# Expert weights of a token stored beside its row and fetched with it, in a kernel of attention and a routed expert layer

## The chip, the cores and the metric

The kernel runs on one core of one Trainium2 chip. The metric is the device time of one execution in microseconds (us).

## What is computed

The input is x, 2 sequences of 2048 tokens with 256 values each, float32. First comes attention with 16 heads of 16 values (softmax over all keys, the causal mask applied after it), added to x and layer-normalised: h. Then the expert layer with 8 experts, two for each token:

```
probs = softmax(h @ router_weight.T);  the two largest, divided by their sum = the weights of a token
each expert keeps at most capacity = 1280 of its tokens, those with the largest weights
kept_w = weight / sum of the kept weights of the token
out[token] = sum over its two experts of kept_w * ((pre * silu(gate)) @ ff_post_act_weight[e].T)
result = layernorm(h + out)
```

With pre and gate the products of the token's row with two 256 x 1024 matrices of the expert.

## The kernel before, in words

**Attention (up to 1034 us of the trace)** is not touched. It leaves x + attention in `x_sb`, 128 partitions by 32 token tiles by 256. Rows of the first sequence are normalised there and stored by SyncE (SP) to `h_dram` (the rows that experts gather) and `acc_dram` (the rows onto which results are added). Both are 4096 x 256 float32.

**Routing (1034 to 1067 us).** ScalarE (ACT) normalises the second sequence and splits the first expert's up weights into two parts for exact products (L1548 on). SP stores the second sequence's rows (L1242, L1243). VectorE (DVE) works through `route` (L1683 on), a chain of small dependent instructions: the two picks of each token (`pick`, one-hot over 8 experts for 32 token tiles), its weights (`kept_w`, L1711), the place of each token in its expert's list (`prefixes`, `places`), and then whether some expert has more than 1280 tokens (`flag`). If it has, a further branch of every engine runs; here it doesn't run. GpSimd (POOL) makes the constant tables, clears a part of y and copies the first expert's down weights (L1288), and then waits.

**The list (1067 to 1094 us).** `slot_row` says for each slot of each expert which token stands in it, 128 partitions by 80 columns (8 experts by 10 tiles of slots); `slot_w` has the token's weight. Both come out of one-hot products, in 8 pieces of 8 token tiles, with two buffers of each operand: DVE makes `in_q` (L1676: which of 80 columns) and `in_p` (L1677: which partition), DVE multiplies `in_q` by the token number into one half of `marks` (L1681), ACT multiplies it by the weight into the other half, eight instructions for a piece (L1536), and TensorE (PE) adds up `in_p` transposed times `marks` (L1388), 128 x 160 float32, eight products of two passes for a piece. The semaphore `list_ready` hands the buffers back to DVE (L1673) and ACT. After piece 8 DVE copies both halves out (L1795, L1796), and POOL, which waits for `slot_row` alone of these (L1309), gathers the first expert's rows with ten indirect DMAs (L1302), 128 rows each. PE begins the first expert when the first four have landed.

**The experts (1109 us to the end).** A loop over eight experts. For each, PE makes the up products in two groups of 512 slots and eight blocks f (L1431), ACT and DVE form the hidden rows, PE makes the down products (L1446), and DVE multiplies them by the slot's weight `wt2` while it copies them out (`leave`, L1866). POOL gathers the next expert's rows at the start of an expert and adds the results onto `acc_dram`. A third group with up to 256 slots runs for experts with over 1024 tokens. DVE sets `wt2` at an expert's start, from ten columns of `slot_w`, once `expert_over` has come (L1875 to L1877). At f = 4 (TURN_AT_F) of the first group, DVE takes the transposed rows of the second group (L1811), and at f = 5 it splits the down weights (L1805). The last expert has a branch of its own that normalises everything and stores it.

Of the kernel before, what the change touches and what calls it, by code (L numbers as in the profile page):

```python
# [4 lines left out]
FP32 = mybir.dt.float32  # L5
# [221 lines left out]
def program(nc, x_tok, x_T, wq, wk, wv, wr_T, w1_T, wg_T, w2_T, out):  # L227
    ctx = ExitStack()
    with ctx:
        def sem(name):  # L230
            return ctx.enter_context(nc.semaphore(name))

        def sb(stack, name, shape, dt=FP32):
            return stack.enter_context(nc.sbuf_tensor(name, shape, dt))
# [7 lines left out]
        v_dram = nc.dram_tensor("v_dram", (NGP, P, NT * VW), FP32).ap()  # L242
        h_dram = nc.dram_tensor("h_dram", (T, D), FP32).ap()
        acc_dram = nc.dram_tensor("acc_dram", (T, D), FP32).ap()
# [454 lines left out]
        acc_view = acc_dram.rearrange("(t p) d -> p t d", p=P)  # L699
        h_view = h_dram.rearrange("(t p) d -> p t d", p=P)  # L700
        stats = ctx.enter_context(nc.sbuf_tensor("stats", [P, TT, 6], FP32, side="right"))
# [48 lines left out]
        with ExitStack() as st, nc.Block() as block:  # L750
# [198 lines left out]
            def _(dve):  # L949
# [79 lines left out]
                for gg in range(NGP):  # L1029
                    for back, work, x, i in DVE_ORDER:  # L1030
# [8 lines left out]
                        if gg >= GPB and back == 0 and work == "sum" and x % 4 == 3 and measured < NT:  # L1039
                            if measured == 0:  # L1040
# [23 lines left out]
        over_ready, cand_ready, cand_count = sem("over_ready"), sem("cand_ready"), sem("cand_count")  # L1064
        places_ready, eq_ready, id_ready, wgt_ready, list_ready = (sem("places_ready"), sem("eq_ready"), sem("id_ready"), sem("wgt_ready"),
                                                                   sem("list_ready"))
        lists_read, more_ready = sem("lists_read"), sem("more_ready")
        PIECES = [(k, part) for part in range(TT // OHP) for k in range(TOPK)]
# [27 lines left out]
        with ExitStack() as st, nc.Block() as block:  # L1096
# [5 lines left out]
            xin_at = nc.sbuf_base  # L1102
            xin = [sb(st, f"xin{j}", [P, CT, D]) for j in range(2)]
            assert xin_at >= probs_at and nc.sbuf_base <= probs_at + 4 * P_RING * KSPAN
            y = [sb(st, f"y{j}", [P, CT, D]) for j in range(2)]
            slot_row = sb(st, "slot_row", [P, NSLOT], U32)
            slot_w = sb(st, "slot_w", [P, NSLOT])
            row = [sb(st, f"row{j}", [P, CT], U32) for j in range(2)]
# [35 lines left out]
            in_q = [sb(st, f"in_q{j}", [P, OHP, NSLOT]) for j in range(2)]  # L1144
            marks = [sb(st, f"marks{j}", [P, OHP, 2, NSLOT]) for j in range(2)]

# [34 lines left out]
            cand_ps = y_ps[:, 2, 0:E]  # L1181
            list_ps = y_ps[:, 3, 0:2 * NSLOT]
# [4 lines left out]
            others = xin[0]  # L1187
# [48 lines left out]
            def _(sp):  # L1236
# [5 lines left out]
                sp.dma_start(h_view[:, of_batch(1), :], x_sb[:, of_batch(1), :]).then_inc(h_stored, 16)  # L1242
                sp.dma_start(acc_view[:, of_batch(1), :], x_sb[:, of_batch(1), :]).then_inc(acc_stored, 16)  # L1243

                def body(i, j, prep):
# [25 lines left out]
            def _(pool):  # L1271
# [13 lines left out]
                def split_down(i, j):  # L1285
                    pool.wait_ge(r2_loaded, count(16, i, j, 16))
                    pool.sem_inc(pool_went_on, 1)
                    nc.gpsimd.tensor_copy(w2[0][:], raw2[:]).then_inc(w2_hi, 1)  # L1288

                split_down(0, 0)  # L1290

                def set_rows(j, e, rows_set):
# [15 lines left out]
                pool.wait_ge(acc_stored, 16 * B)  # L1308
                pool.wait_ge(lists_read, 1)  # L1309
                fetch(0, slot_row[:, 0:CT])  # L1310
# [70 lines left out]
            def _(pe):  # L1381
                def list_piece(n, round):

                    pe.wait_ge(id_ready, n + 1 + round * NP)
                    if round == 0:
                        pe.wait_ge(wgt_ready, OHP * (n + 1))
                    for t in range(OHP):
                        last = nc.tensor.matmul(list_ps, in_p[n % 2][:, t, :], marks[n % 2][:, t, :, :].rearrange("p v s -> p (v s)"),  # L1388
                                                start=(n == 0 and t == 0), stop=(t == OHP - 1), skip_group_check=True)
                    last.then_inc(list_ready, 1)  # L1390
# [120 lines left out]
            def _(act):  # L1511
# [17 lines left out]

                def weights(n):  # L1530
                    k, tiles = of_piece(n)
# [18 lines left out]
                for n in range(2 * DC):  # L1550
                    split_up_piece(n)
                for n in range(NP):
                    weights(n)

# [61 lines left out]
            def _(dve):  # L1616
# [51 lines left out]
                def mark(n, round):  # L1668

                    k, tiles = of_piece(n)  # L1670
                    at = n + round * NP
                    if at >= 2:
                        dve.wait_ge(list_ready, at - 1)  # L1673
                        if round == 0:
                            dve.wait_ge(wgt_ready, OHP * (at - 1))
                    nc.vector.tensor_tensor(in_q[n % 2][:], each(upward[:, 0:NSLOT], tiles), wide(at_q[:, k, tiles], NSLOT), ALU.is_equal).then_inc(eq_ready, 1)  # L1676
                    nc.vector.tensor_tensor(in_p[n % 2][:], each(upward, tiles), wide(at_p[:, k, tiles], P), ALU.is_equal)  # L1677
                    dve.wait_ge(eq_ready, at + 1)
                    if round == 1:
                        nc.vector.tensor_tensor(marks[n % 2][:, :, 1, :], in_q[n % 2][:], wide(kept_w[:, k, tiles], NSLOT), ALU.mult)  # L1680
# [62 lines left out]
                with dve.If(too_many > 0):  # L1743
                    link5 = chain(dve, dve5)

                    link5(nc.vector.tensor_tensor(wm[:], pick[0][:], wide(wgt[:, 0, :]), ALU.mult))
                    link5(nc.vector.tensor_tensor(work[:], pick[1][:], wide(wgt[:, 1, :]), ALU.mult))
# [40 lines left out]
                    weigh(link5, kept_w, kept_w, ALL)  # L1788
                    places(link5, ALL)
                    dve.wait_ge(places_ready, 2)  # L1790
# [79 lines left out]
                dve.wait_ge(y_cleared, 2)  # L1870
                dve.wait_ge(wt_set, 1)

                def body(i, j, prep):

                    dve.wait_ge(expert_over, i * 2 + (j + 1))  # L1875
                    nc.vector.tensor_copy(wt2[j][:], slot_w[:, bass.ds((i * 2 + j) * CT, CT)]).then_inc(wt_set, 1)
                    dve.wait_ge(wt_set, i * 2 + (j + 2))  # L1877
                    for g in range(2):
# [23 lines left out]
                        for f in range(FC + 1):  # L1902
# [72 lines left out]
```

## Time and profile before

| | |
|---|---|
| median of three runs | 1734.03 us (1733.4 to 1735.66) |
| the profiled execution's own time | 1735.2 us |
| its span in the trace | 1733.4 us |
| PE busy | 1622.3 us (94%) |
| ACT busy | 1255.3 us (72%) |
| DVE busy | 1141.7 us (66%) |
| POOL busy | 300.2 us (17%) |

The span is from the first to the last record of the trace; the 1.8 us between it and the time lie around it. Busy shares are averages over stages that have different limits, so the argument is made in the stages that the change touches, from the instructions in order of time. A "chain" is the sequence of work that ended last, followed back from the end.

### The profile page before, as it was taken

The numbers are of one execution on the slowest core, as the hardware profiler recorded it, in microseconds if no ns is written. First come the engines' busy times: TensorE is split into PE (matmuls) and PEld (weight loads), VectorE is DVE, ScalarE is ACT, GpSimd is POOL, SyncE is SP. The second block draws the span as 40 slices with busy tenths as digits, with TensorE's granted clock in tenths as the row PEclk, the third lists the DMA queues.
The fourth block names the chain that finished last, engine by engine and source line by source line (L and its number), as shares of the span: only waits on it lengthen the run. The fifth ranks groups of instructions, "written<-read, shape, count | busy, mean of one in ns | idle before, by whom it ended". The sixth has DMA issues, their size and how long they took to land. (4 is left out here: it accounts for less than half of the span.)

```text
span 1733.4 us, 31338 instructions
## 1 busy us (share of the span) xinstructions
PE 1622.3 (94%) x12878; PEld 951.5 (55%) x12878; DVE 1141.7 (66%) x1766; ACT 1255.3 (72%) x1350; POOL 300.2 (17%) x247
## 2 busy tenths in 40 slices
PE   8979999999999999999999993699999999999995
PEld 6723333333333333333333343589998988889984
DVE  7847687777776878777868778445454444644474
ACT  7869999999999999999999985233333333433333
POOL 1000000000000000000310000424243425425144
PEclk9979999999999999999999996899999999999998
DMA  7692030300300303003031002213142323323043
GB/s 258 209 256 67 1 88 1 78 11 2 88 1 1 88 1 78 11 2 88 1 100 48 1 26 97 98 38 107 15 112 65 69 57 68 100 50 90 5 134 121
DMA packets 78897, 118.29 MB, mean 68 GB/s; under 512 B 9202, under 2 KB 62811, under 8 KB 78734
## 3 DMA queue, kind: packets, MB, share of 16 engines
q1 hardware_dynamic: 63840, 98.32, 19.2%
q0 software_dynamic: 14880, 17.82, 5.8%
q8 instruction: 109, 1.79, 0.4%
q14 instruction: 36, 0.29, 0.1%
q10 hardware_dynamic: 32, 0.07, 0.0%
HBM read 80.22 MB, written 40.37 MB: 70 GB/s over the span
## 5 line engine op out<-in xcount | busy, mean ns | idle before, releaser
L973 DVE TENSOR_REDUCE sums<-expq 128x1 f32<-128x1536 f32 (+7 forms) x576 | 559.6, 1033 | 175.7 <-ACT expq L943 175.3
L943 ACT ACTIVATE probs<-scores 128x1536 f32<-128x1536 f32 (+1 forms) x384 | 509.2, 1478 | 12.3 <-PE scores L839 12.0
L943 ACT ACTIVATE expq<-scores 128x1536 f32<-128x1536 f32 x320 | 447.4, 1536 | 2.5 <-PE scores L839 0.9
L861 PE MATMUL o_ps<-probs,v 128*32 128x256 f32 (+1 forms) x4864 | 347.8, 368 | 0.0
L839 PE MATMUL scores<-aq,ak 98*128 98x512 bf16 (+3 forms) x1280 | 304.2, 353 | 12.4 <-PEq L620 10.9
L1594 ACT ACTIVATE gate<-up_ps 128x512 f32<-128x512 f32 x128 | 76.6, 599 | 326.3 <-PE up_ps L1431 315.7
L839 PE MATMUL scores<-ak,aq 98*128 98x512 bf16 (+3 forms) x1184 | 265.1, 343 | 22.7 <-ACT probs L943 16.9
L839 PEld LDWEIGHTS scores<-aq,ak 98*128 98x128 bf16 x1280 | 95.1, 98 | 216.6 <-ACT expq L943 75.5
L1431 PE MATMUL up_ps<-xeT_hi,wup_hi 128*128 128x512 f32 x512 | 202.9, 396 | 3.3 <-DVE xeT_lo L1811 1.4
L1907 DVE TENSOR_TENSOR mid<-up_ps,gate 128x512 f32<-128x512 f32 x128 | 88.4, 691 | 176.1 <-ACT gate L1594 171.0
L1431 PE MATMUL up_ps<-xeT_lo,wup_hi 128*128 128x512 f32 x512 | 202.5, 395 | 0.0
L1431 PE MATMUL up_ps<-xeT_hi,wup_lo 128*128 128x512 f32 x512 | 201.5, 393 | 0.0
L839 PEld LDWEIGHTS scores<-ak,aq 98*128 98x128 bf16 x1184 | 88.7, 98 | 198.8 <-ACT probs L943 91.0
L861 PEld LDWEIGHTS o_ps<-probs,v 128*32 128x32 f32 x4864 | 100.1, 108 | 170.0 <-issue 168.5
L1446 PE MATMUL y_ps<-w_hi,mid_hi 128*128 128x256 f32 x528 | 148.2, 281 | 0.0
L1446 PE MATMUL y_ps<-w_lo,mid_hi 128*128 128x256 f32 x528 | 147.5, 279 | 0.0
L1446 PE MATMUL y_ps<-w_hi,mid_lo 128*128 128x256 f32 x528 | 147.3, 279 | 0.0
L811 POOL TENSOR_TENSOR x_sb<-x_sb,attn 128x1024 f32<-128x1024 f32 x7 | 16.6, 2374 | 744.6 <-DVE attn L1004 744.6
L1352 POOL DMA_INDIRECT acc_dram<-y,row x70 | 110.0, 1571 | 126.6 <-DVE y L1866 80.4
L1431 PEld LDWEIGHTS up_ps<-xeT_hi,wup_hi 128*128 128x128 f32 x512 | 96.8, 189 | 25.5 <-DVE xeT_lo L1811 1.8
L1431 PEld LDWEIGHTS up_ps<-xeT_hi,wup_lo 128*128 128x128 f32 x512 | 96.8, 189 | 21.1
L1431 PEld LDWEIGHTS up_ps<-xeT_lo,wup_hi 128*128 128x128 f32 x512 | 96.7, 189 | 21.2
(268 smaller groups left out, 1903.6 us busy)
## 6 DMA issues: line engine op xcount, KB each, us to landing
raw<-w_T SPq DMA_DIRECT2D x16, 1024.0 KB
split_dram<-parts SPq DMA_DIRECT2D x48, 256.0 KB, 2.9
aq<-split_dram SPq DMA_DIRECT2D x42, 256.0 KB
ak<-split_dram SPq DMA_DIRECT2D x42, 256.0 KB
raw<-wg_T SPq DMA_DIRECT2D x8, 1024.0 KB
v_dram<-vst SPq DMA_DIRECT2D x8, 544.0 KB, 4.7
v<-v_dram SPq DMA_DIRECT2D x8, 544.0 KB, 10.6
xT<-x_T SPq DMA_DIRECT2D x8, 512.0 KB, 6.2
```

Of the source, the lines that this page charges most:

```text
L811: nc.gpsimd.tensor_tensor(cols, cols, attn[:], ALU.add).then_inc(attn_added, 1)
L839: last = nc.tensor.matmul(dst[:, at:at + w], still, moving[0:KS, h, lo:lo + w], start=True, stop=True, skip_group_check=True)
L861: last = nc.tensor.matmul(o_ps[g % O_RING][32 * h:32 * h + 32, col:col + w], value(gg, k, h, 32), probs[:, m % 2 * GH + h, at:at + w], sta ...
L943: nc.scalar.activation(dst, src[:, 0:w], ACT.Exp, scale=HD ** -0.5).then_inc(exp_done, 1)
L973: last = nc.vector.tensor_reduce(sums[:, gg % 2, col, h:h + 1], expq[:, at % X_RING, lo:lo + w], AX.X, ALU.add)
L1352: pool.indirect_dma_start(out=acc_dram[:, :], out_offset=bass.IndirectOffsetOnAxis(ap=row[j][:, t:t + 1], axis=0), in_=y[j][:, t, :], in_o ...
L1431: last = nc.tensor.matmul(up_ps[n % 2][:, k, 0:cols.stop - cols.start], wup[a][:, k, c, f * P:(f + 1) * P], x[b][:, c, cols], start=(c == ...
L1446: last = nc.tensor.matmul(y_ps[:, t, :], mid2[a][:, f, t * P:(t + 1) * P], w2[b][:, f, :], start=(f == 0 and t % 2 == 0 and (a, b) == PAIR ...
L1594: nc.scalar.activation(gate[f % 2][:], up_ps[f % 2][:, 0, :], ACT.Silu).then_inc(silu_done, 1)
L1907: nc.vector.tensor_tensor(mid[f % 2][:], up_ps[f % 2][:, 1, :], gate[f % 2][:], ALU.mult).then_inc(mul_done, 1)
```

## The change

`h_dram` gets eight more columns: a row is 264 values, 1056 bytes. The kept weights of a token are spread over eight columns by expert (`dense`), which takes three instructions on POOL, and one further DMA of SP writes them beside the rows, 4096 pieces of 32 bytes. A gathered row then brings its weight with it, and `wt2` is taken from the gathered tile, at f = 4 instead of at the expert's start. The list's products carry the token numbers alone, 80 columns instead of 160; ACT makes them in place of the weights, and DVE no longer multiplies. The first gather waits for `slot_row` and, through SP, for the weights to be in memory. The diff, cut to its core; what is left out besides is the branch for an expert with too many tokens, which does the same for its own weights:

```diff
-        h_dram = nc.dram_tensor("h_dram", (T, D), FP32).ap()
+        h_dram = nc.dram_tensor("h_dram", (T, D + E), FP32).ap()
...
-        h_view = h_dram.rearrange("(t p) d -> p t d", p=P)
+        h_rows = h_dram.rearrange("(t p) d -> p t d", p=P)
+        h_view, w_view = h_rows[:, :, 0:D], h_rows[:, :, D:D + E]
...
-            xin = [sb(st, f"xin{j}", [P, CT, D]) for j in range(2)]
+            xin = [sb(st, f"xin{j}", [P, CT, D + E]) for j in range(2)]
...
-            marks = [sb(st, f"marks{j}", [P, OHP, 2, NSLOT]) for j in range(2)]
+            marks = [sb(st, f"marks{j}", [P, OHP, NSLOT]) for j in range(2)]
+            dense, dense_1 = sb(st, "dense", [P, TT, E]), sb(st, "dense_1", [P, TT, E])
...
@@ SyncE, behind the stores of the second sequence's rows @@
+                sp.wait_ge(dense_ready, 4)
+                sp.dma_start(w_view, dense[:]).then_inc(h_stored, 16)
+                sp.wait_ge(over_ready, 1)
+                too_many = sp.value_load(flag[0:1, 1:2], min_val=0, max_val=1)
+                sp.wait_ge(h_stored, 16 * (B + 1))
...
+                sp.sem_inc(rows_known, 1)
...
@@ GpSimd, behind the copy of the first down weights @@
+                pool.wait_ge(dense_ready, 1)
+                nc.gpsimd.tensor_tensor(dense[:], pick[0][:], wide(kept_w[:, 0, :]), ALU.mult).then_inc(dense_ready, 1)
+                nc.gpsimd.tensor_tensor(dense_1[:], pick[1][:], wide(kept_w[:, 1, :]), ALU.mult).then_inc(dense_ready, 1)
+                pool.wait_ge(dense_ready, 3)
+                nc.gpsimd.tensor_tensor(dense[:], dense[:], dense_1[:], ALU.add).then_inc(dense_ready, 1)
...
-                pool.wait_ge(lists_read, 1)
+                pool.wait_ge(rows_known, 2)
                 fetch(0, slot_row[:, 0:CT])
...
@@ TensorE, list_piece @@
-                    pe.wait_ge(id_ready, n + 1 + round * NP)
-                    if round == 0:
-                        pe.wait_ge(wgt_ready, OHP * (n + 1))
+                    pe.wait_ge(at_ready, n + 1 + round * NP)
+                    pe.wait_ge(id_ready, OHP * (n + 1 + round * NP))
                     for t in range(OHP):
-                        last = nc.tensor.matmul(list_ps, in_p[n % 2][:, t, :], marks[n % 2][:, t, :, :].rearrange("p v s -> p (v s)"),
+                        last = nc.tensor.matmul(list_ps, in_p[n % 2][:, t, :], marks[n % 2][:, t, :],
...
@@ ScalarE, mark_ids in place of weights @@
-                        nc.scalar.activation(marks[n % 2][:, t, 1, :], in_q[n % 2][:, t, :], ACT.Copy,
-                                             scale=kept_w[:, k, tiles.start + t:tiles.start + t + 1]).then_inc(wgt_ready, 1)
+                        nc.scalar.activation(marks[n % 2][:, t, :], in_q[n % 2][:, t, :], ACT.Copy,
+                                             scale=ids[:, tiles.start + t:tiles.start + t + 1]).then_inc(id_ready, 1)
...
@@ VectorE, mark @@
-                    nc.vector.tensor_tensor(in_p[n % 2][:], each(upward, tiles), wide(at_p[:, k, tiles], P), ALU.is_equal)
-                    dve.wait_ge(eq_ready, at + 1)
+                    nc.vector.tensor_tensor(in_p[n % 2][:], each(upward, tiles), wide(at_p[:, k, tiles], P), ALU.is_equal).then_inc(at_ready, 1)
...
-                    nc.vector.tensor_tensor(marks[n % 2][:, :, 0, :], in_q[n % 2][:], wide(ids[:, tiles], NSLOT), ALU.mult).then_inc(id_ready, 1)
@@ VectorE, route @@
                     weigh(link, kept_w, wgt, tiles)
+                    dve.sem_inc(dense_ready, 1)
                     upto_tile = prefixes(link, 1, tiles)
@@ VectorE, behind the list @@
-                nc.vector.tensor_scalar(slot_row[:], list_ps[:, 0:NSLOT], float(T), None, ALU.add).then_inc(lists_read, 1)
-                nc.vector.tensor_copy(slot_w[:], list_ps[:, NSLOT:2 * NSLOT]).then_inc(wt_set, 1)
+                nc.vector.tensor_scalar(slot_row[:], list_ps[:, 0:NSLOT], float(T), None, ALU.add).then_inc(rows_known, 1)
@@ VectorE, experts @@
                     dve.wait_ge(expert_over, i * 2 + (j + 1))
-                    nc.vector.tensor_copy(wt2[j][:], slot_w[:, bass.ds((i * 2 + j) * CT, CT)]).then_inc(wt_set, 1)
-                    dve.wait_ge(wt_set, i * 2 + (j + 2))
...
                             if g == 0 and f == TURN_AT_F:
+                                dve.wait_ge(xrest_loaded[j], i * (16 * (CT - NA)) + 16 * (CT - NA))
+                                nc.vector.tensor_copy(wt2[j][:, :, None], xin[j][:, :, bass.ds(i * 2 + (D + j), 1)]).then_inc(wt_set, 1)
                                 turn_lo(i, j, 1)
...
+                        dve.wait_ge(wt_set, i * 2 + (j + 1))
                         dve.wait_ge(y_ready, count(2, i, j, g + 1))
```

## Rows read from the trace of the kernel before

**Rows 1.** The page: busy time of the engines.

```profile
PE 1622.3 (94%) x12878; PEld 951.5 (55%) x12878; DVE 1141.7 (66%) x1766; ACT 1255.3 (72%) x1350; POOL 300.2 (17%) x247
```

**Rows 2.** The chain in order of time, list to first expert: start us, us, what.

```profile
1090.89 2.43 PE y_ps L1388 x16
...
1093.89 0.23 DVE slot_row L1795
...
1109.82 13.22 PE up_ps L1431 x48
```

**Rows 3.** Instructions in order of time, routing: start us, us, engine, line, what, count.

```profile
1057.25 0.22 DVE L1636 TENSOR_TENSOR kept_w<-wgt,tmp 128x64 f32<-128x64 f32 x1
1057.66 0.42 DVE L1643 COPY tot<-y_ps 128x256 f32<-128x256 f32 x1 [0.18 <-PE y_ps L1378]
```

**Rows 4.** The same view, the list: first piece, then the fifth and sixth begin.

```profile
1066.94 0.80 DVE L1676 TENSOR_TENSOR in_q<-upward,at_q 128x640 f32<-128x640 f32 x1
1070.05 6.08 PE L1388 MATMUL y_ps<-marks,in_p 128*128 128x160 f32 x32 [12.49 <-ACT marks L1536]
...
1079.57 0.83 DVE L1676 TENSOR_TENSOR in_q<-upward,at_q 128x640 f32<-128x640 f32 x1 [0.28 <-PE y_ps L1388]
1080.43 2.13 ACT L1536 ACTIVATE marks<-in_q,kept_w 128x80 f32<-128x80 f32 x8 [0.85 <-DVE in_q L1676]
1081.45 0.82 DVE L1681 TENSOR_TENSOR marks<-in_q,ids 128x640 f32<-128x640 f32 x1
1082.71 2.41 PE L1388 MATMUL y_ps<-marks,in_p 128*128 128x160 f32 x16 [0.57 <-ACT marks L1536]
...
1085.15 0.82 DVE L1676 TENSOR_TENSOR in_q<-upward,at_q 128x640 f32<-128x640 f32 x1 [0.28 <-PE y_ps L1388]
```

**Rows 5.** Stretches of the list: busy (count) by engine, then PEclk, DMA share, GB/s.

```profile
1069.90:1073.05 3.15, 3.00 (x11) 3.04 (x12) 0.80 (x1) 2.13 (x9) 0.50 0.01 3
1073.05:1093.40 20.35, 17.54 (x119) 16.03 (x117) 4.91 (x6) 12.76 (x48) 1.00 0.01 2
```

**Rows 6.** PE: narrow products in order of time, and durations (min/median/max ns) by tile.

```profile
114.77 0.61 PE L890 MATMUL o_ps<-wr,ones 128*128 128x8 f32 x4
...
1106.44 1.97 PE L1423 MATMUL xt_ps<-ident,xin 128*128 128x128 f32 x8 [13.14 <-DMA xin<-h_dram,slot_row]
...
L890 PE MATMUL o_ps<-wr,ones x4: 256/256/277, 114.8 to 115.1; 128*128 128x8 f32 x4
L1388 PE MATMUL y_ps<-marks,in_p x128: 299/299/605, 1070.0 to 1093.0; 128*128 128x160 f32 x128
```

**Rows 7.** POOL's copy beside DVE in order of time; POOL's tensor_tensor (min/median/max ns).

```profile
1040.45 1.89 POOL L1288 CAST w_hi<-raw 128x2048 fp32r<-128x2048 f32 x1 [3.46 <-DMA raw<-w_T]
1040.63 1.74 DVE L198 TENSOR_TENSOR tmp<-tmp 128x16 f32<-128x16 f32 x1
...
L811 POOL TENSOR_TENSOR x_sb<-x_sb,attn x7: 2366/2373/2381, 228.3 to 921.2; 128x1024 f32<-128x1024 f32 x7
```

**Rows 8.** 1056 to 1068 (as rows 5), its packets; those of 107.8:108.2; smallest DMA.

```profile
1056.00:1068.00 12.00, 1.55 (x4) 0.67 (x2) 10.86 (x45) 2.47 (x4) 0.00 (x0) 0.50 1.01 334
...
DMA packets 3946, 4.01 MB, mean 334 GB/s; under 512 B 32, under 2 KB 3946, under 8 KB 3946
...
q1 hardware_dynamic: 97, 0.01, 15.2%
...
wr<-wr_T SPq DMA_DIRECT2D x1, 8.0 KB, 2.3
```

**Rows 9.** Stretch of the first gathers, as rows 5.

```profile
1100.00:1106.40 6.40, 0.00 (x0) 0.00 (x0) 0.00 (x0) 0.00 (x0) 5.00 (x5) 0.50 0.99 360
```

**Rows 10.** DVE in the experts, in order of time.

```profile
1182.04 0.56 DVE L1876 COPY wt<-slot_w 128x10 f32 x1
1183.89 0.69 DVE L1907 TENSOR_TENSOR mid<-up_ps,gate 128x512 f32<-128x512 f32 x1 [1.29 <-ACT gate L1594]
...
1360.31 0.69 DVE L1907 TENSOR_TENSOR mid<-up_ps,gate 128x512 f32<-128x512 f32 x1 [0.81 <-ACT gate L1594]
```

More of the change, by code:

```diff
@@ L1064, in program @@
         over_ready, cand_ready, cand_count = sem("over_ready"), sem("cand_ready"), sem("cand_count")
-        places_ready, eq_ready, id_ready, wgt_ready, list_ready = (sem("places_ready"), sem("eq_ready"), sem("id_ready"), sem("wgt_ready"),
-                                                                   sem("list_ready"))
-        lists_read, more_ready = sem("lists_read"), sem("more_ready")
+        places_ready, eq_ready, id_ready, at_ready, list_ready = (sem("places_ready"), sem("eq_ready"), sem("id_ready"), sem("at_ready"),
+                                                                  sem("list_ready"))
+        dense_ready = sem("dense_ready")
+        rows_known, more_ready = sem("rows_known"), sem("more_ready")
         PIECES = [(k, part) for part in range(TT // OHP) for k in range(TOPK)]
@@ L1102, in program @@
             xin_at = nc.sbuf_base
-            xin = [sb(st, f"xin{j}", [P, CT, D]) for j in range(2)]
-            assert xin_at >= probs_at and nc.sbuf_base <= probs_at + 4 * P_RING * KSPAN
+            xin = [sb(st, f"xin{j}", [P, CT, D + E]) for j in range(2)]
+            assert xin_at >= probs_at and nc.sbuf_base <= probs_at + 4 * (P_RING + X_RING) * KSPAN
             y = [sb(st, f"y{j}", [P, CT, D]) for j in range(2)]
             slot_row = sb(st, "slot_row", [P, NSLOT], U32)
-            slot_w = sb(st, "slot_w", [P, NSLOT])
             row = [sb(st, f"row{j}", [P, CT], U32) for j in range(2)]
@@ L1181, in program @@
             cand_ps = y_ps[:, 2, 0:E]
-            list_ps = y_ps[:, 3, 0:2 * NSLOT]
+            list_ps = y_ps[:, 3, 0:NSLOT]
             last_ps = [y_ps[:, 0, :], xt_ps[0][:, 0:D], y_ps[:, 2, :], xt_ps[1][:, 0:D]]
@@ L1186, in program @@
             room = [raw1[:].rearrange("p k c f -> p (k c f)").rearrange("p (t d) -> p t d", d=D), y[0], raw2]
-            others = xin[0]
+            others = xin[0][:, :, 0:D]
             PAIRS = ((0, 0), (1, 0), (0, 1))
@@ L1243, in _ @@
                 sp.dma_start(acc_view[:, of_batch(1), :], x_sb[:, of_batch(1), :]).then_inc(acc_stored, 16)
+                sp.wait_ge(dense_ready, 4)
[3 more added lines that the diff above has]
+                sp.wait_ge(h_stored, 16 * (B + 1))
+                with sp.If(too_many > 0):
+                    sp.wait_ge(dense_ready, 5)
+                    sp.dma_start(w_view, dense[:]).then_inc(h_stored, 16)
+                    sp.wait_ge(h_stored, 16 * (B + 2))
+                sp.sem_inc(rows_known, 1)
                 def body(i, j, prep):
@@ L1528, in normalise_h, with mark_ids @@
                     nc.scalar.activation(x_sb[:, t, :], x_sb[:, t, :], ACT.Identity, bias=nbias[:, t:t + 1], scale=rstd[:, t:t + 1]).then_inc(h_by_act, 1)
-                def weights(n):
-                    k, tiles = of_piece(n)
+                def mark_ids(n):
+                    tiles = of_piece(n)[1]
                     act.wait_ge(eq_ready, n + 1)
@@ L1551, in _ @@
                     split_up_piece(n)
+                act.wait_ge(iota_ready, 8)
                 for n in range(NP):
-                    weights(n)
+                    mark_ids(n)
                 turn_hi(0, 0, 0)
@@ L1674, in mark @@
                         if round == 0:
-                            dve.wait_ge(wgt_ready, OHP * (at - 1))
+                            dve.wait_ge(id_ready, OHP * (at - 1))
                     nc.vector.tensor_tensor(in_q[n % 2][:], each(upward[:, 0:NSLOT], tiles), wide(at_q[:, k, tiles], NSLOT), ALU.is_equal).then_inc(eq_ready, 1)
-                    nc.vector.tensor_tensor(in_p[n % 2][:], each(upward, tiles), wide(at_p[:, k, tiles], P), ALU.is_equal)
-                    dve.wait_ge(eq_ready, at + 1)
+                    nc.vector.tensor_tensor(in_p[n % 2][:], each(upward, tiles), wide(at_p[:, k, tiles], P), ALU.is_equal).then_inc(at_ready, 1)
                     if round == 1:
-                        nc.vector.tensor_tensor(marks[n % 2][:, :, 1, :], in_q[n % 2][:], wide(kept_w[:, k, tiles], NSLOT), ALU.mult)
-                    nc.vector.tensor_tensor(marks[n % 2][:, :, 0, :], in_q[n % 2][:], wide(ids[:, tiles], NSLOT), ALU.mult).then_inc(id_ready, 1)
+                        dve.wait_ge(eq_ready, at + 1)
+                        nc.vector.tensor_tensor(marks[n % 2][:], in_q[n % 2][:], wide(ids[:, tiles], NSLOT), ALU.mult).then_inc(id_ready, OHP)
                 def route():
@@ L1744, in _ @@
                     link5 = chain(dve, dve5)
+                    dve.wait_ge(dense_ready, 4)
                     link5(nc.vector.tensor_tensor(wm[:], pick[0][:], wide(wgt[:, 0, :]), ALU.mult))
@@ L1788, in _ @@
                     weigh(link5, kept_w, kept_w, ALL)
+                    dve.wait_ge(h_stored, 16 * (B + 1))
+                    link5(nc.vector.tensor_tensor(dense[:], pick[0][:], wide(kept_w[:, 0, :]), ALU.mult))
+                    link5(nc.vector.tensor_tensor(dense_1[:], pick[1][:], wide(kept_w[:, 1, :]), ALU.mult))
+                    nc.vector.tensor_tensor(dense[:], dense[:], dense_1[:], ALU.add).then_inc(dense_ready, 1)
                     places(link5, ALL)
@@ L1870, in _ @@
                 dve.wait_ge(y_cleared, 2)
-                dve.wait_ge(wt_set, 1)
                 def body(i, j, prep):
                     dve.wait_ge(expert_over, i * 2 + (j + 1))
-                    nc.vector.tensor_copy(wt2[j][:], slot_w[:, bass.ds((i * 2 + j) * CT, CT)]).then_inc(wt_set, 1)
-                    dve.wait_ge(wt_set, i * 2 + (j + 2))
                     for g in range(2):
```

## The prediction, made before the changed kernel was run

> **What bounds the kernel now.** I read the page first [rows 1]: PE is busy for 94% of the span, but that is an average. The chain [rows 2] shows one stretch around the change where PE isn't the limit: the list's products end at 1093.3, DVE copies `slot_row` at 1093.89, and PE's next large group begins only at 1109.82. From there to about 1668 the chain is PE nearly throughout. So whatever shifts the moment at which `slot_row` is ready shifts the end by as much, and what DVE, POOL and SP do inside the expert loop is hidden as long as PE doesn't wait for it.
>
> Then I read the routing and the list instruction by instruction [rows 3, 4]. The last weights (`kept_w`) end at 1057.47; a chain of DVE instructions runs to the first `in_q` at 1066.94. In the list two buffers go round. Fifth piece: `in_q` at 1079.57, ACT from 1080.43 for 2.13, PE from 1082.71 for 2.41, and at 1085.15 the next `in_q` into the same buffer, released by PE. So two pieces take 5.58 us: 3.14 from `in_q` to PE's start, 2.41 of PE and 0.03. DVE's multiplication (L1681) [rows 4] isn't in that sequence; ACT and PE are.
>
> **The change, part by part.**
>
> *PE's products, 80 columns for 160.* Sixteen passes take 2.41 us, the last one 0.30 of it [rows 6], so they start every 0.14 us. Halving the columns doesn't halve this, because 128 columns of weights are loaded for each pass: the four 128 x 8 products took 0.61 us with the last at 0.26 [rows 6], so (0.61 - 0.26) / 3 = 0.117, at the full clock. Taken as 0.11 to 0.12 for 80 columns: 15 x 0.11 + 0.27 = 1.92 us, 0.49 less. The other bound is half of 0.14, 15 x 0.07 + 0.27 = 1.3 us. I take 1.92, since eight columns already cost as much.
>
> *ACT* keeps eight instructions of the same shape for a piece; only the scale operand differs. Cost: nothing.
>
> *DVE* loses eight multiplications of 0.82. The second `in_q` of a pair can start when `in_p` is done, 1.88 us after the first (1079.57 to 1081.45) [rows 4] instead of some 2.6. ACT can't use all of this: its second piece starts when the first ends, 2.99 after the first `in_q`, and ends at 5.12; PE takes it at 5.27 to 7.2. That is no bound beyond the first chain: a pair then takes 3.14 + 1.92 + 0.03 = 5.09 us.
>
> Played through: `in_q` 0 at 1066.94; PE starts its first piece at 1070.05 as before. There the clock is 0.50 for 3.0 us [rows 5], eleven passes at 0.27. With 128 weight columns and 128 moving ones passes started every (1.97 - 0.47) / 7 = 0.21 us at that clock [rows 6], where 0.47 for the last is an estimate, not quite twice the 0.26. So the first piece takes 3.0 us + 2 passes = 3.4 for 3.9: 0.5 less. Two further rounds of 5.09 for 5.58 on the even side: 1.0. The last pair, with `in_q` 7 2.15 us after `in_q` 6 for 2.62 and PE's last piece: 0.5 + 0.5. **Sum: 2.4 us less** (bounds 0, if ACT or the semaphores pace it anyway, and 4.0, with the short pass).
>
> *The three POOL instructions.* 128 x 1024 took 2.37 us in this form [rows 7]; a quarter of it, with some 0.17 of fixed part, is 0.17 + 2.2 / 4 = 0.72 each, 2.2 in all, from about 1057.7. POOL has nothing else then, but DVE has. At 1040.63 a DVE tensor_tensor of 16 columns took 1.74 us, where one of 64 takes 0.22 (L1636) [rows 3], and it ended with POOL's copy, which had started 0.18 before it [rows 7]. So DVE's two-input instructions stop while POOL reads and writes. Behind `kept_w` stands nothing but such a chain. Its first member reads PSUM (L1643) [rows 3] and takes 0.42; the rest is blocked. Cost on the path: 2.2 - 0.4 = **1.7 us more** (bounds 0 and 2.2; 0 if DVE always wins). The Trainium skill, SBUF — State Buffer, "Who interferes with whom", has the rule behind this: a VectorE instruction with two SBUF inputs contends with a GpSimd one that reads SBUF, whichever is first blocks the other. By it the instruction from PSUM escapes (the 1.7); by the row alone the sum would be 2.2.
>
> *SP's DMA and its waits.* `dense` is ready at about 1060.5. SP has issued both stores by 1056.84 and its queue is full: 3946 packets fill all engines from 1056 to 1068 [rows 8], 12 / (3946 / 16) = 0.049 us for a packet of 1 KB on an engine. The 4096 pieces of 32 bytes come behind them. Their price isn't in the trace: the nearest rows are small packets read at 107.8 to 108.2, 0.4 x 16 x 0.152 / 97 = 0.010 us each [rows 8], and the 1 KB stores themselves, 0.049. That gives 256 x 0.010 = 2.6 to 256 x 0.049 = 12.5 us; I take the upper, the only writes among them. With rows that now start at odd multiples of 32 bytes the stores may end at 1069 to 1070. The smallest DMA took 2.3 us from issue to landing [rows 8]; with 2 for that end they have landed by 1070 + 12.5 + 2 = 1084.5. `slot_row` is ready at 1094.1 - 2.4 + 1.7 = 1093.4. So SP's sem_inc is 9 us early, and POOL's wait is free. Behind SP's wait stands only the load of the second expert's up weights, issued at 1099. Cost: nothing. If the cover goes, every us past 1093 is a us of the kernel.
>
> *DVE's sem_inc* in the chain: 0.05 us. *Wider rows:* a gather moves 3% more. The first four land while the DMA engines are 99% busy until 1106.4 with the second expert's weights [rows 9]; 0.1 us more (bounds 0 and 1). `slot_w`'s copy stood behind `slot_row` and its own followers weren't late: nothing.
>
> *`wt2` at f = 4.* The copy before took 0.56 at an expert's start, and DVE idled 1.29 behind it [rows 10]: its loss brings nothing. In its new place it comes ahead of 1.28 us of L1811 and 2.28 of L1805; DVE catches up by f = 7, where it still idled 0.81 for ACT [rows 10], so the 0.56 fits. Seven loops the same: nothing. Its cover is that 0.81.
>
> **Sum:** -2.4 + 1.7 + 0.05 + 0.1 = -0.6 us, from the profiled execution's 1735.2 to 1734.6. That execution is 1.2 above the median, 1734.03, so the median becomes 1733.4. A comparison here can tell about 0.2%, 3.5 us, from no change.
>
> **The rivals.**
>
> *PE and DVE give more.* If an 80-column pass starts every 0.07 to 0.08, each of the pairs loses a further 0.5, and if POOL's instructions wait for DVE rather than DVE for them, the 1.7 is gone: -4.0, to 1730.0. For it: halved columns. Against it: rows 6 and rows 7.
>
> *The weights land too late (the other side).* Place: POOL's first gather. It decides when a 32-byte write takes over (1093.4 - 2 - 1070) / 256 = 0.084 us; the result is beyond 0.2% at 0.10. For it: pieces far below a row, at a stride of 1056 bytes, in one DMA of 4096. Against it: small reads cost a fifth of a 1 KB write [rows 8]. At twice the 1 KB price, 0.098, they land at 1070 + 25 + 2 = 1097; at 0.12, at 1103: 4 to 9 us late, so 1737 to 1743, at the middle 1740. The Trainium skill, DMA: Bandwidth & Descriptors, "Specifications", says that below 512 bytes the engine does read-modify-write; no row here shows its price, and it is the reason why this case isn't smaller.
>
> *PE stays at half clock in the list.* It is at 0.50 until 1073.05 and then 1.00 [rows 5], with PE busy 17.54 of 20.35. With shorter pieces it is busy some 75%. At 0.50 a piece takes 15 x 0.21 + 0.47 = 3.6, PE is the bound, and eight take 29 for 23.3 now: 5.7 more, 1741.5. Against it: the first piece still fills the time in which the clock rose.
>
> *The change does nothing for the list:* ACT paces it, -0, and DVE's block stays: 1735.8; inside 0.2%.
>
> **How the numbers follow.** The forecast, with its bounds: 0.72 together with the last case. More gain: 0.14. Late weights: 0.10. Half clock: 0.04. So faster 0.14, same 0.72, slower 0.14. The forecast's own bounds, -4.0 to +2.4 or so, give 1730 to 1736.5; to take in the nearer part of the late weights I go to 1738.
>
> **What would show it.** Right: passes of L1388 starting 0.11 apart, 1.9 us for a piece; in_q at a pair distance of 5.1; DVE instructions of 0.5 to 0.9 us with POOL's three beside them at 1058 to 1060, and first `in_q` at 1068.6; `slot_row` near 1093.3; SP's DMA landed before 1086; POOL's gather 1 us behind `slot_row`. Wrong: a gather that waits for DMA or SP; PEclk under 1.00 after the first pieces; PE gaps in the loop at f = 6 or 7, waiting for DVE; gathers over 1.0 us each.

## The result, and the profile after

The changed kernel took 1744.15 us (median of four runs, 1743.21 to 1745.02) against 1734.85 for the kernel before beside it: ratio 1.0055, 95% interval 1.0043 to 1.0067, so 9.3 us slower. Forecast was 1733.4, in a range of 1730 to 1738.

The stage of the change in the changed kernel, instructions in order of time (columns as in [rows 3]); lines have moved, L1693 is the old L1676, L1404 the old L1388, L1552 the old L1536, L1817 the old L1795:

```profile
1057.03 0.22 DVE L1653 TENSOR_TENSOR kept_w<-wgt,tmp 128x64 f32<-128x64 f32 x1
1057.40 0.63 POOL L1304 TENSOR_TENSOR dense<-pick,kept_w 128x256 f32<-128x256 f32 x1 [15.27 <-DVEq L1728]
1057.99 0.87 POOL L1305 TENSOR_TENSOR dense<-pick,kept_w 128x256 f32<-128x256 f32 x1
1058.41 0.48 DVE L1663 COPY cs<-cs 128x16 f32<-128x16 f32 x1
1058.94 0.84 POOL L1307 TENSOR_TENSOR dense<-dense 128x256 f32<-128x256 f32 x1
1059.24 0.58 DVE L1663 COPY cs<-cs 128x32 f32<-128x32 f32 x1
1059.81 2.96 SPq L1247 DMA_DIRECT2D h_dram<-dense  x1
...
1067.42 0.80 DVE L1693 TENSOR_TENSOR in_q<-upward,at_q 128x640 f32<-128x640 f32 x1
1070.58 27.61 PE L1404 MATMUL y_ps<-marks,in_p 128*128 128x80 f32 x128 [13.25 <-ACT marks L1552]
1077.71 0.83 DVE L1693 TENSOR_TENSOR in_q<-upward,at_q 128x640 f32<-128x640 f32 x1 [1.45 <-PE y_ps L1404]
1081.14 0.82 DVE L1693 TENSOR_TENSOR in_q<-upward,at_q 128x640 f32<-128x640 f32 x1 [1.47 <-PE y_ps L1404]
1098.78 0.24 DVE L1817 TENSOR_SCALAR slot_row<-y_ps 128x80 uint32<-128x80 f32 x1 [5.43 <-PE y_ps L1404]
```

The view merged all 128 product passes of the list into one row of 27.61 us, because no pause lies between them: PE works without a break. A piece, and with it an `in_q`, now comes every 3.42 us, where one came every 2.79 us, half of the 5.58 us of a pair [rows 4]. The clock of the same stretches, columns as in [rows 5], PEclk third from the end:

```profile
1070.50:1074.00 3.50, 3.42 (x16) 3.45 (x17) 0.72 (x1) 1.96 (x8) 0.00 (x0) 0.50 0.01 2
1074.00:1098.30 24.30, 24.19 (x114) 23.98 (x113) 11.76 (x12) 12.75 (x48) 0.00 (x0) 0.50 0.01 1
```

Before, the clock went from 0.50 to 1.00 at 1073.05 [rows 5]. Now it is at 0.50, which is 1.2 GHz, to the last product. A pass starts every 27.6 / 128 = 0.216 us.

A second loss sits where nothing was forecast. Pieces of the chain in order of time, first of the kernel before, then of the changed one (start us, us, what; the 48 are the first up products of the first expert, the 96 the up products of the second group of the first two experts):

```profile
1146.26 21.98 PE up_ps L1431 x96
1232.20 21.98 PE up_ps L1431 x96
```

```profile
1114.76 12.72 PE up_ps L1447 x48
1150.99 22.31 PE up_ps L1447 x96
1237.63 22.31 PE up_ps L1447 x96
```

The same products start every 0.2324 us for 0.2290. The 8.1 us by which the spans differ (1741.5 and 1733.4) lie here:

| stretch | changed, us | before, us | difference |
|---|---|---|---|
| start of the span to the start of `kept_w` | 1057.03 | 1057.25 | -0.22 |
| `kept_w` to the first `in_q` | 10.39 | 9.69 | +0.70 |
| first `in_q` to `slot_row` (the list) | 31.36 | 26.95 | +4.41 |
| `slot_row` to the first up product | 15.98 | 15.93 | +0.05 |
| first up product to the end of the span | 626.74 | 623.58 | +3.16 |

### The profile page after: what moved, and what is told of

Read it like the earlier page. It is cut to its first block and busy times, and to the rows that moved or that the text cites. A ratio compares the mean times of both kernels' runs of the same rounds, so it can differ in the third digit from the quotient of the medians.

```text
span 1741.5 us, 31340 instructions
## 1 busy us (share of the span) xinstructions
PE 1634.0 (94%) x12878; PEld 960.2 (55%) x12878; DVE 1135.0 (65%) x1757; ACT 1254.9 (72%) x1350; POOL 304.2 (17%) x250
```

## The experiments

Theory A: the narrow products leave PE at half clock in the list (B in the expectations is its rival). Theory C (its rival is D): the second loss is one of address. The change widens `xin` by 640 bytes of each partition and drops `slot_w` with 320, so all tiles behind them lie 320 bytes further on, among them the transposed rows (`xeT_hi`, `xeT_lo`), which the up products stream. Their start goes from byte 138080 to 138400 of a partition. Rivals: another part of the change holds the clock down; the wider rows or their DMAs slow the loop; POOL's three instructions beside DVE's chain account for more than 0.7. The kernel before beside them took 1734.6 us in the first batch (e1 to e4) and 1729.4 to 1729.8 in the later ones (e6 to e13), so ratios are compared, not times. The traces show where nearly all of these 5 us lie: from the last expert's second 48 up products to the end of the span it is 76.0 to 77.0 us in all six traces of the first batch and 71.4 to 72.9 in all eight later ones, behind everything that is argued here. A reading from such rows is taken from one trace for each kernel.

**e1_wide**

```diff
-            marks = [sb(st, f"marks{j}", [P, OHP, NSLOT]) for j in range(2)]
+            marks = [sb(st, f"marks{j}", [P, OHP, 2 * NSLOT]) for j in range(2)]
...
-            list_ps = y_ps[:, 3, 0:NSLOT]
+            list_ps = y_ps[:, 3, 0:2 * NSLOT]
...
+                for j in range(2):
+                    pool.memset(marks[j][:], 1.0).then_inc(marks_set, 1)
```

Left out: ACT still writes only the first 80 columns of `marks`, and waits once for POOL's constant. The address of `xeT` stays where the change put it.

> The changed kernel, but its list products have 160 columns again: the token numbers in the first 80, the constant 1.0 in the others; nobody reads those. Theory A (clock): the list took 27.6 us because PE stayed at half clock, and it stayed there because the narrow products kept it less loaded. With 160 columns the clock rises 3 us after the first product, a piece takes 2.4 us, slot_row is ready near 1094.4 us of the trace instead of 1099.0, and the time falls by 4.5 to 5 us, to 1739.5. Rival B (PE's wait, or the operand ACT writes now, holds the clock down whatever the width): wider products at half clock take 16 x 0.27 = 4.3 us a piece, slot_row comes at 1106, the time rises by 7.

Measured: 1739.9 us, ratio 1.0031 (1.0019 to 1.0044). `slot_row` at 1095.66, where 1094.4 was expected. In order of time, the first two pieces and the third:

```profile
1070.82 7.51 PE L1406 MATMUL y_ps<-marks,in_p 128*128 128x160 f32 x32 [13.28 <-ACT marks L1554]
1078.60 2.41 PE L1406 MATMUL y_ps<-marks,in_p 128*128 128x160 f32 x16 [0.27 <-ACT marks L1554]
```

Doubling the columns shortened the piece from 3.42 to 2.41 us. Rival B of the expectation, 7 us more, is out. The expectation missed when the clock rises:

```profile
1076.50:1077.00 0.50, 0.50 (x4) 0.50 (x4) 0.50 (x1) 0.50 (x3) 0.00 (x0) 0.71 0.00 0
```

It rose in this stretch, 6 us after the first product, where it took 3 us in the kernel before, so the first two pieces took 7.51 us for 6.08. That is what is left of the list's loss (28.03 us from the first `in_q` to `slot_row`, 26.95 before); why the clock rose later isn't shown.

**e2_xt_back** and **e3_before_xt**: only the place of `xeT_hi`, `xeT_lo` and the tiles right behind them (`xeTC`, `gate`, `mid`), in the changed kernel and in the one before. 704 bytes make the shift 1024 in all.

```diff
-            spot = {"x": x_at, "route": -(-(route_at + 32) // 64) * 64 - 32}
+            spot = {"x": x_at, "route": -(-(route_at + 32) // 64) * 64 - 32 + 704}
```

(320 in place of 704 for the kernel before.)

> The changed kernel with the transposed rows and what lies behind them (xeT_hi, xeT_lo and so on) placed 704 bytes further on, so that their address modulo 1024 is what it was in the kernel before; nothing else. Theory C (address): some 3 us of the loss are up products that start every 0.2324 us instead of 0.2290 in the second group, because the change moved these tiles by 320 bytes. Then 96 of them take 21.98 us again instead of 22.31, and the time falls by 3 us, to 1741. Rival D (the spacing comes from something else, the wider gathered rows or the DMA beside them): 22.31 stays, 1744.

> The kernel before with the same tiles placed 320 bytes further on, where the change puts them; nothing else. Theory C: the up products of the second group go from 21.98 to 22.31 us per 96, and the time rises by 3 us, to 1738. Rival D: 1735, no difference.

Measured: e2_xt_back 1738.84 us, ratio 1.0026 (1.0016 to 1.0035); e3_before_xt 1738.86 us, ratio 1.0026 (1.0016 to 1.0036). Pieces of the chain of e2_xt_back, then of e1_wide, which kept the new address, then of e3_before_xt; the `up_ps` rows are the second group of the first expert:

```profile
1069.48 27.62 PE y_ps L1404 x128
1149.76 21.99 PE up_ps L1447 x96
```

```profile
1081.50 2.42 PE y_ps L1406 x16
1147.54 22.30 PE up_ps L1449 x96
```

```profile
1146.16 22.30 PE up_ps L1431 x96
```

In these pieces, moving the tiles alone takes the kernel before to 22.30 and the changed kernel back to 21.99, with its list untouched at 27.62. But a single piece is no safe sign of the address: other groups of e2_xt_back took 22.41, and so did the first expert's second group in three runs with the tiles at their old place modulo 1024 (22.40 in e10_before_narrow, e11_wide_xt_warm and e13_narrow_held):

```profile
1234.66 22.41 PE up_ps L1447 x96
...
1151.27 22.40 PE up_ps L1431 x96
```

(The first row is of e2_xt_back, the second of e10_before_narrow.) What separates the two places without exception is the whole loop, from the first expert's first 96 down products to the last expert's second 48 up products. Its two ends, in the kernel before and in the changed one:

```profile
1134.95 11.31 PE y_ps L1446 x96
...
1657.21 11.02 PE up_ps L1431 x48
```

```profile
1139.68 11.31 PE y_ps L1462 x96
...
1665.11 11.19 PE up_ps L1447 x48
```

The time between the starts of these two:

| place of `xeT` | traces | us |
|---|---|---|
| old, or old + 1024 | before, e2, e6, e7, e10 to e13 | 518.4 to 522.3 |
| + 64, + 128, + 320 | changed kernel, e1, e3, e4, e8, e9 | 525.3 to 525.9 |

The kernel before goes from 522.3 to 525.7 by the move (e3_before_xt), the changed kernel from 525.4 to 520.4 (e2_xt_back). So rival D of the expectation is out. The prices, 4.2 and 5.3 us by the medians, are above the 3 expected, and these 3.5 and 5.0 us of the loop are most of them. At the old place the loop varies by 3.9 us between traces; what sets that isn't shown.

**e4_warm**

```diff
                 prefix_products(ALL).then_inc(prefix_ready, 1)
+                for n in range(12):
+                    nc.tensor.matmul(up_ps[0][:, 0, :], ones[:], after[:].rearrange("p a b -> p (a b)"), start=True, stop=True)
```

> The changed kernel with twelve products of 128 x 512 float32 on constants put on PE ahead of the list, in the 13 us in which it idles between the prefix products and the first piece; their result is not read. Theory A: PE is at full clock when the list begins. If the clock then holds through the list's pauses, a piece takes 1.9 us, a pair 5.1, slot_row comes near 1090.5, and the time falls by 8 us, to 1736. If it falls back because the narrow products are too light, the list begins fast and ends slow, between 1092 and 1099. If the first of these, being cold, makes no difference at all, 1744: then it isn't the clock at the start.

Measured: 1742.92 us, ratio 1.0044 (1.0031 to 1.0058). Its list in three stretches:

```profile
1061.00:1071.90 10.90, 9.15 (x22) 3.78 (x20) 10.21 (x36) 2.19 (x9) 0.17 (x1) 1.00 0.92 261
1071.90:1077.90 6.00, 4.74 (x39) 4.53 (x40) 4.56 (x5) 4.99 (x21) 0.00 (x0) 1.00 0.00 1
1078.00:1097.00 19.00, 19.00 (x90) 18.94 (x89) 7.84 (x8) 9.50 (x36) 0.00 (x0) 0.50 0.01 2
```

The list begins at full clock, two pieces in 4.00 us. Then PE pauses for 1.15 us, and at 1078, 0.9 us into the third piece, the clock falls to 0.50. It doesn't rise again while the narrow products last, though PE is busy 19.00 of 19.00 us. This is the middle case of the expectation: the narrow products didn't raise the clock, and with their pauses they didn't hold it.

**e10_before_narrow**: in the kernel before, one part of the change alone. The weights are made but not summed, and `slot_w` gets the token numbers in their place, so this kernel leaves out the right scaling of the results. All else is as in the kernel before.

```diff
-            list_ps = y_ps[:, 3, 0:2 * NSLOT]
+            list_ps = y_ps[:, 3, 0:NSLOT]
...
-                        last = nc.tensor.matmul(list_ps, in_p[n % 2][:, t, :], marks[n % 2][:, t, :, :].rearrange("p v s -> p (v s)"),
+                        last = nc.tensor.matmul(list_ps, in_p[n % 2][:, t, :], marks[n % 2][:, t, 0, :],
```

> The kernel before with one part of the change alone: the list's products take the 80 columns of token numbers; the weights are still made, but not summed, and slot_w gets the token numbers in their place, so that results are scaled wrongly. Theory A (the width alone keeps the clock down): PEclk stays at 0.50 through the list, each piece takes 3.4 us, slot_row comes 4 to 4.5 us later, 1738.8. Rival (the clock stayed down because ACT's and PE's rhythm or SP's stores changed): the clock rises at the third microsecond and the time falls by 2, to 1732.5.

Measured: ratio 1.0026 (1.0016 to 1.0036), 1734.04 us against 1729.8. Clock of the list, and its products in order of time:

```profile
1070.00:1074.00 4.00, 4.00 (x21) 4.00 (x20) 2.46 (x4) 1.92 (x8) 0.00 (x0) 0.50 0.01 2
1074.00:1098.00 24.00, 23.06 (x108) 22.84 (x107) 15.69 (x20) 12.76 (x48) 0.00 (x0) 0.50 0.00 1
```

```profile
1069.45 27.61 PE L1388 MATMUL y_ps<-marks,in_p 128*128 128x80 f32 x128 [12.49 <-ACT marks L1536]
```

27.61 us, as in the changed kernel, without any other part of it. The width alone does it.

**e6_wide_xt**: the edits of e1_wide and e2_xt_back together.

> Both mends at once in the changed kernel: list products of 160 columns, and the transposed rows at their old address modulo 1024. If the clock in the list and the address are the two causes and nothing else is left, their gains add: 1744.2 - 4.3 - 5.3 = 1734.6, the time before. If a third cause is left (the port, the weights' DMA, the wider rows), it stays above 1736.

Measured: 1731.36 us against 1729.8, ratio 1.0006 (0.9997 to 1.0015). The two mends give 0.0024 and 0.0029 of 0.0055 alone, and 0.0049 together. What is left, 0.0006, can't be told from nothing.

**e8_before_64** and **e9_before_128**: as e3_before_xt, with 64 and 128.

> The kernel before with the transposed rows 64 bytes further on. A shift of 320 bytes cost it 4.2 us; 320 differs from no shift in the 64s and in the 256s. If the 64s decide (address modulo 128), this costs 4 us too, 1739, with 22.3 us per 96 products of the second group. If the 256s decide, 1734.6 and 21.98.

> The kernel before with the transposed rows 128 bytes further on. If the address modulo 128 decides, nothing changes: 1734.6. If this is slower as well, it is no matter of one bit but of where each tile lies against the weights.

Measured: ratios 1.0034 (1.0022 to 1.0046) and 1.0031 (1.002 to 1.0042). By the chain, 96 products of the second group take 22.3 us with 64 and 22.4 with 128 (0.2323 and 0.2332 us a product), and the loop 525.7 and 525.3 us. So it is neither the 256s alone nor the address modulo 128: all three shifts tried, 64, 128 and 320, are slower, and only the shift of 1024 brought the loop back. What the rule is, and which operand the tiles disturb, stays open.

**e7_before_warm**: the twelve products of e4_warm in the kernel before, and thirteen like them between the list and the first expert.

> The kernel before with PE kept at work in its two idle stretches: twelve products of 128 x 512 on constants ahead of the list, thirteen between the list and the first expert, their result not read. Theory A says that the list then begins at full clock (first piece 2.4 us for 3.9) and so does the first expert (its first 48 up products in 11.2 us for 13.2): 1.5 + 2 = 3.5 us less, ratio 0.998. If the clock falls in the last idle microsecond ahead of either, or PE isn't what the first piece waits for, there is no gain.

Measured: 1724.82 us against 1729.82, ratio 0.997 (0.9957 to 0.9982). The list starts at full clock; the first piece, from the chain:

```profile
1070.54 2.42 PE y_ps L1388 x16
...
1108.20 12.65 PE up_ps L1433 x48
```

2.42 for 3.9 us, as expected. The first 48 up products gained 0.6 us only (13.22 before [rows 2]), not 2. The clock shows why (columns as in [rows 5], with POOL's busy time ahead of PEclk):

```profile
1104.00:1106.00 2.00, 0.47 (x4) 0.47 (x5) 0.00 (x0) 0.00 (x0) 1.39 (x3) 1.00 1.02 381
...
1108.00:1110.00 2.00, 1.80 (x4) 1.49 (x5) 0.24 (x2) 0.61 (x1) 0.78 (x3) 0.50 0.02 0
```

The thirteen products were over at 1103.5, PE then had only the transposes of the gathered rows to do, 1.1 us, and the clock was back at 0.50 when the up products began.

The part from the first up product to the end of the span is 1722.7 - 1108.20 = 614.5 us for 623.58. Of these 9 us, 4.6 are the end of the span, which is shorter in every trace of the later batches, and 0.6 are the first 48. The other 3.9 lie in the loop (518.4 for 522.3), long after the added products. So of the 5.0 us that the medians give, the list has 1.5 (25.45 us from the first `in_q` to `slot_row`, 26.95 before) and the way from there through the first expert's first two times 48 up products 1.2; the rest falls in the loop, and that the added products cause it isn't shown.

**e11_wide_xt_warm** and **e12_late_dense**: e6_wide_xt with the twelve products; and with the thirteen and this edit besides.

```diff
                 pool.wait_ge(dense_ready, 1)
+                pool.wait_ge(at_ready, 2)
                 nc.gpsimd.tensor_tensor(dense[:], pick[0][:], wide(kept_w[:, 0, :]), ALU.mult).then_inc(dense_ready, 1)
```

> The changed kernel with list products of 160 columns, the old address modulo 1024, and the twelve products ahead of the list. Against the same without the twelve (ratio 1.0006) the list's first two pieces should fall from 7.5 us to 4.9, and nothing else change: 2.5 us less, ratio 0.999.

> As the one before, with the thirteen products ahead of the first expert as well, and with POOL's three instructions held back until DVE has made the in_p of the second piece, so that they no longer run beside DVE's chain. If these three are what made the way from kept_w to the first in_q 10.2 us instead of 9.5, it is 9.5 again; the weights' DMA then lands near 1078 of the trace, before slot_row, and costs nothing. With 2 us for the first expert: ratio 0.9975. If the way stays 10.2, the port isn't its cause.

Measured: e11_wide_xt_warm 1.0 (0.9991 to 1.001), e12_late_dense 0.9968 (0.9956 to 0.9981), 1724.91 against 1729.82. In the first, the list from first `in_q` to `slot_row` took 25.11 us for 27.76 in e6_wide_xt, as expected; by the ratios (1.0 and 1.0006) this gain can't be told from nothing. In the second, in order of time:

```profile
1056.24 0.22 DVE L1661 TENSOR_TENSOR kept_w<-wgt,tmp 128x64 f32<-128x64 f32 x1
1065.90 0.80 DVE L1701 TENSOR_TENSOR in_q<-upward,at_q 128x640 f32<-128x640 f32 x1
1069.86 0.63 POOL L1307 TENSOR_TENSOR dense<-pick,kept_w 128x256 f32<-128x256 f32 x1 [28.53 <-DVE in_p L1702]
...
1071.53 1.03 DVE L1701 TENSOR_TENSOR in_q<-upward,at_q 128x640 f32<-128x640 f32 x1 [1.83 <-PE y_ps L1407]
```

9.66 us from `kept_w` to `in_q`, where it was 10.39 with POOL's instructions beside the chain and 9.69 before. So they cost 0.7 us there, and held back some 0.2: the `in_q` at 1071.53 took 1.03 us for 0.82, and the list 25.30 us for 25.11.

**e13_narrow_held**: the changed kernel with its narrow products, all the other mends, and

```diff
                     last.then_inc(list_ready, 1)
+                    if round == 0 and n < NP - 1:
+                        nc.tensor.matmul(up_ps[0][:, 0, 0:256], ones[:], after[:, 0:2, :].rearrange("p a b -> p (a b)"), start=True, stop=True)
```

> The changed kernel with its 80-column products, the old address modulo 1024, POOL's three instructions held back, the twelve and thirteen products on constants in PE's idle stretches, and besides one product of 128 x 256 on constants behind each piece of the list but the last, 0.4 us in PE's pause. It asks what the narrow products would have given with the clock up. If the added load holds PEclk at 1.00, a piece takes 1.9 to 2.0 us, a pair 5.1 instead of 5.6, the list ends some 2 us earlier than with 160 columns (ratio 0.9968), and the ratio is 0.9957. If the clock falls in spite of it, the list takes up to 27 us again, and the ratio is near 0.9985.

Measured: ratio 0.9972 (0.9961 to 0.9983), 1724.91 us against 1729.45. Two pieces in order of time, and a stretch of the list:

```profile
1080.84 1.98 PE L1405 MATMUL y_ps<-marks,in_p 128*128 128x80 f32 x16 [0.29 <-ACT marks L1559]
1082.66 0.64 PE L1409 MATMUL up_ps<-after,ones 128*128 128x256 f32 x2
1083.24 1.98 PE L1405 MATMUL y_ps<-marks,in_p 128*128 128x80 f32 x16
1085.99 1.98 PE L1405 MATMUL y_ps<-marks,in_p 128*128 128x80 f32 x16 [0.29 <-ACT marks L1559]
```

```profile
1080.00:1084.00 4.00, 3.71 (x28) 3.02 (x28) 3.10 (x4) 3.10 (x13) 0.00 (x0) 1.00 0.02 4
```

The clock holds: in this stretch PE did the narrow products and the added ones. A piece takes 1.98 us and a pair 5.15 (1080.84 to 1085.99); `in_q` to `slot_row` is 23.60 us for 25.30 in e12_late_dense. Most of these 1.7 us doesn't reach the loop: the first 48 up products took 13.99 us for 12.84, because the clock was at 0.50 until about 1112 here and until about 1110 there, and why isn't shown. The ratio expected was 0.9957, and the one measured can't be told from 0.9968 of e12_late_dense. So the narrow list is faster if something else keeps the clock up, by 1.7 us against the wide one with a warm start; no time here shows the gain.

## Why the prediction was wrong

**The step that failed** is the term "PE's products, 80 columns for 160", with its play-through. It took the first piece at 3.4 us, and all further ones at 1.92, at full clock, as if the clock's rise at 1073 belonged to the stage and not to what PE did in it. The runs show in its place a clock that stays at 0.50 through all eight pieces, at 3.42 us each. The price of a pass was right: 0.11 at full clock ((1.98 - 0.3) / 15 in e13_narrow_held), 0.216 at half, for 0.21 forecast. But the narrow products didn't get to full clock by themselves in any run: not in the changed kernel, e2_xt_back or e10_before_narrow, nor in e4_warm once it had fallen; in e13_narrow_held added products keep it up. The list became 4.4 us longer instead of 2.4 shorter (e1_wide, e4_warm, e10_before_narrow). The Trainium skill, TensorE: Matmul & The Clock Gate, "LDWEIGHTS (loading the stationary operand)", gives P / 1.2 nanoseconds for P weight columns, 107 for 128; the 0.11 at full clock agrees, the 0.216 at half clock is twice that.

**The rival "PE stays at half clock in the list"** is what happened, and I gave it 0.04. Its price was right in kind: 3.6 us a piece forecast, 3.42 measured. Its reason was not: it had PE busy for only some 75%, and PE was busy for 24.19 of 24.30 us. What I held against it, that the first piece still fills the time in which the clock rose, was no evidence either: PE did fill that time, and the clock stayed at 0.50 for all 27.6 us of the list. Busy time in the trace didn't say what the clock would do; the width of the products did.

**No term at all** stood for the address of `xeT`. The diff shows both sizes that move it, and the sum said of the loop that it changes nothing. It was 3.2 us of the trace, a third of the loss, and 3.5 to 5.0 us of the loop in e3_before_xt and e2_xt_back.

**POOL's three instructions** cost 0.7 us (10.39 - 9.69, and gone in e12_late_dense) for 1.7. That one engine waits for the other was right; that DVE does all the waiting was wrong. POOL's first ran beside DVE's copy from PSUM and took 0.63 us; its next two, each begun while one of DVE's two-input instructions ran, took 0.87 and 0.84. Those two-input instructions kept their 0.40 us. What grew were DVE's copies of 16 and 32 columns, 0.48 and 0.58 us where they took 0.17 and 0.18, and each ended when POOL's instruction did (1058.89 and 1058.86, 1059.82 and 1059.78). The two copies are 0.71 us longer together, which is the whole cost. So the rows fit engines that wait for the rest of each other's instruction, in turn, and not a DVE that waits for all three of POOL's.

**SP's DMA** was in time, as forecast, by far more. Packets in the changed kernel from 1068 to 1070 us:

```profile
DMA packets 3243, 0.11 MB, mean 56 GB/s; under 512 B 3242, under 2 KB 3242, under 8 KB 3242
```

with a DMA share of 0.72: an estimate from it is 2 x 16 x 0.72 / 3243 = 0.007 us for a 32-byte write on an engine, near the small reads' 0.010 [rows 8] and not the 0.049 I took. The stores of whole rows were through before 1068, all 4096 small writes by 1070, and the DMA landed 11.2 us after its issue, at 1071.0, 28 us before `slot_row`. So the rival on the other side, which needed 0.084 us for a write, was wrong. It leaned on the Trainium skill, DMA: Bandwidth & Descriptors, "Specifications", which says that below 512 bytes the engine does read-modify-write; whether it does isn't shown here, but a 32-byte write took a seventh of the time of a 1 KB one, if over four times as much for each byte.

**The rest held.** Gathers of 1056 bytes took POOL 0.998 us each at the median, as before 1.002; `slot_row` to the first product 15.98 for 15.93. `wt2` at f = 4 costs DVE some 0.2 us, and DVE still idled 0.88 at f = 7. By the spans the forecast was -0.6 and the result +8.1. Of the 8.7 us between, the list is 6.8, the address 3.2 and POOL's instructions -1.0. The upper end of the range came from the DMA's rival and not from the clock's; the list's loss alone would have passed it.

## What to carry to other kernels

Where PE's clock is still low, ask of every change that makes its products smaller whether the clock will rise at all: here half the columns for the same number of weight loads took 4.4 us longer. A change that resizes a tile also moves every tile allocated behind it; compare their addresses before and after, and put the streamed operands back where they were before anything is concluded from the time. Compare whole stages for it: single groups of products took 21.98 or 22.40 us at the same address. Some 12 products on constants in PE's idle stretch ahead of a short PE stage can start it at full clock, if they end close before it (1.8 us in e4_warm): they took 1.5 us off the first piece (e7_before_warm), while after the thirteen, which ended 4.7 us ahead of the first expert's up products, the clock was down again. With 25 of them the kernel before (e7_before_warm) and the changed one with its other mends (e12_late_dense) ran 0.3% faster than the kernel before. About half of that, 2.7 of 5.0 us in e7_before_warm, lies in the stages at which they aim; the rest isn't explained.

## What the runs showed of the hardware that was not expected

PE's clock stayed at 0.50 through 27.6 us of 128 x 80 products without a pause (the changed kernel, e2_xt_back, e10_before_narrow), and in e4_warm it fell from 1.00 to 0.50 at 1078, 0.9 us into the third piece of them, behind a pause of 1.15 us. In e1_wide, 128 x 160 products in the same place raised it. The loop of up and down products took 525.3 to 525.9 us with the streamed tiles 64, 128 or 320 bytes further on, and 518.4 to 522.3 us with a shift of 0 or 1024 bytes. Beside POOL's tensor_tensors, DVE's copies of 16 and 32 columns took 0.48 and 0.58 us for 0.17 and 0.18, and ended within 0.04 us of them. And 4096 writes of 32 bytes, at a stride of 1056, cost some 0.007 us each on an engine.
